# Two output projections and the first tile's normalisation moved into the last two half periods of the attention

## What is computed

```python
mod = (silu(c) @ wmod)                      # six vectors per batch: sa, ca, ga, sb, cb, gb
h = layernorm(x) * (1 + ca) + sa
x = x + ga * (causal_attention(h @ wq, h @ wk, h @ wv, rotary, 32 heads of 32) @ wo)
h = layernorm(x) * (1 + cb) + sb
g = softmax(h @ W_gate.T) - 0.125 * sigmoid(h @ W_thr + b_thr)   # 8 experts
w = where(g >= 0, g, 0); w = w / sum(w)
y = h @ W_base.T + b_base + 2 * einsum('ner,ne,eor->no', h @ A_w, w, B_w)
x = x + gb * y
```

## Time and profile before

| | us |
|---|---|
| median of 3 runs (1678.32 to 1681.45) | 1680.01 |
| the profiled execution: its own time | 1680.86 |
| its span, first to last instruction | 1679.1 |
| TensorE busy (95% of the span) | 1591.7 |
| ScalarE busy (62%) | 1038.7 |
| VectorE busy (57%) | 965.4 |
| Pool busy (36%) | 606.3 |

### The profile page before, as it was taken

How to read it: one execution, slowest core, us unless ns; L and a number is a source line. 1 busy time by engine, 2 the same in 40 slices (tenths; PEclk the granted TensorE clock), 3 DMA queues, 4 the chain that set the end, 5 groups by cost and what they waited for, 6 DMA issues and landing times.

```text
span 1679.1 us, 29431 instructions
## 1 busy us (share of the span) xinstructions
PE 1591.7 (95%) x9530; PEld 1179.7 (70%) x9530; DVE 965.4 (57%) x2916; ACT 1038.7 (62%) x2672; POOL 606.3 (36%) x475
## 2 busy tenths in 40 slices
PE   4899999999999989999999999998789999999996
PEld 2556767667677757777777777764468888888885
DVE  5627577676766646666566557565544545453533
ACT  2347888889889868898898898888621111110100
POOL 3533253453533414334234233231314343434332
PEclk9999999999999989999999999996999999999998
DMA  9673443445433383243233323323641212111110
GB/s 350 217 252 86 110 106 104 123 119 139 117 98 97 75 266 88 58 105 77 74 89 75 91 70 92 78 49 99 171 141 38 75 44 69 51 63 60 53 62 25
DMA packets 172163, 174.44 MB, mean 104 GB/s; under 512 B 21172, under 2 KB 120804, under 8 KB 172024
## 3 DMA queue, kind: packets, MB, share of 16 engines
q1 hardware_dynamic: 169912, 168.55, 35.8%
q10 hardware_dynamic: 2112, 4.19, 0.8%
HBM read 96.65 MB, written 25.18 MB: 73 GB/s over the span
## 4 chain that ended last, share of the span: by engine, by line
PE 80%; DVE 6%; DMA 4%; ACT 4%; issue 3%; POOL 2%; SPq 1%; DVEq 0%; ACTq 0%; POOLq 0%
PE ps_s L1224 14%; PE ps_qkv L1224 13%; PE ps_s L687 10%; PE ps_s L1266 9%; PE ps_pv L1293 9%; PE ps_t L1235 8%; PE ps_s L648 3%; PE ps_s L649 3%; PE ps_s L650 3%; DVE rows_sb L1742 1%; PE ps_qkv L689 1%; DMA x_start<-in_L_attn_x_dram 1%; PE ps_s L1137 1%; ACT probsT L1511 1%; DVE h_pair L1711 1%
## 5 line engine op out<-in xcount | busy, mean ns | idle before, releaser
L1475 ACT ACTIVATE rows_sb<-rows_sb,bias_m 128x640 f32<-128x640 f32 (+7 forms) x512 | 396.1, 774 | 12.4
L1742 DVE CUSTOM_DVE_ANT_0 rows_sb<-ps_t,mask 128x512 f32<-128x512 f32 (+3 forms) x512 | 296.7, 586 | 165.1 <-PE ps_t L1235 157.7
L1511 ACT ACTIVATE probsT<-ps_s 128x512 f32<-128x512 f32 (+2 forms) x640 | 320.9, 542 | 26.3 <-PE ps_s L1266 13.5
L1235 PE MATMUL ps_t<-stk 96*128 96x512 f32 (+3 forms) x768 | 270.2, 355 | 11.6 <-DVE smax L1742 7.8
L1266 PE MATMUL ps_s<-stk 98*128 98x512 f32 (+3 forms) x768 | 230.7, 381 | 7.8 <-ACT probsT L1511 7.4
L1768 DVE TENSOR_TENSOR ps_s<-ps_s,mask_t 128x128 f32<-128x128 f32 (+1 forms) x384 | 120.8, 340 | 170.7 <-PE ps_s L1266 166.8
L1266 PEld LDWEIGHTS ps_s<-stk 98*128 98x128 f32 x768 | 129.9, 193 | 93.0 <-issue 50.5
L1235 PEld LDWEIGHTS ps_t<-stk 96*128 96x128 f32 x768 | 147.4, 192 | 62.8 <-DVE smax L1742 14.4
L1293 PE MATMUL ps_pv<-probsT,v_all 128*32 128x256 f32 (+1 forms) x2816 | 185.0, 357 | 0.9 <-ACT probsT L1511 0.9
L1896 POOL TENSOR_TENSOR rope_b<-rope_b,rope_sin 128x512 f32<-128x512 f32 x64 | 82.8, 1294 | 282.6 <-DVE rope_b L1727 282.6
L1224 PE MATMUL ps_qkv<-hT_hi,w_hi 128*128 128x512 f32 x384 | 159.1, 414 | 12.0 <-DMA hT_lo<-h_scratch 6.8
(11 more groups left out here) (212 smaller groups left out, 3046.0 us busy)
## 6 DMA issues: line engine op xcount, KB each, us to landing
stk<-rot SPq DMA_DIRECT2D x384, 128.0 KB, 2.4
probsT<-in_L_wmod_dram SPq DMA_DIRECT2D x5, 2048.0 KB, 10.6
wm_one<-in_L_wmod_dram SPq DMA_DIRECT2D x5, 2048.0 KB, 14.3
w_raw<-in_L_attn_wq_dram SPq DMA_DIRECT2D x16, 512.0 KB, 4.1
w_raw<-in_L_attn_wk_dram SPq DMA_DIRECT2D x16, 512.0 KB, 4.8
w_raw<-in_L_attn_wv_dram SPq DMA_DIRECT2D x16, 512.0 KB, 4.1
attn_scratch<-attn_sb SPq DMA_DIRECT2D x128, 64.0 KB, 3.0
h_scratch<-h_pair SPq DMA_DIRECT2D x32, 256.0 KB, 3.0
```

The source lines that it names most:

```text
L1235: pe.matmul(bank[:, 0:c1 - c0], stk[0:3 * HD, u % 2, 0, qt // 4, h, qt % 4 * P:(qt % 4 + 1) * P], stk[0:3 * HD, u % 2, 1, part, h, 0:c1 - ...
L1475: act.activation(row, row, ACT.Exp, bias=bias_m[:, qt, h:h + 1], scale=SCALE, accum_out=sums[:, qt // 4, h, qt % 4:qt % 4 + 1]).then_inc(s ...
L1511: act.activation(probsT[:, w % 4, hs[0]:hs[-1] + 1, 0:n], s_bank[(NS * u + k) % 3][:, 0:len(hs) * n].rearrange("p (h n) -> p h n", h=len(hs)),
L1742: dve.tensor_tensor_reduce(rows_sb[:, to, at + c0:at + c1], bank[:, 0:n], mask[:, BANK - n:BANK] if last else mask[:, 0:1].broadcast_to([P ...
```

## The change

- Projection 0 stands in six steps, (30, 6) to (30, 11), 8 matmuls each, projection 1 in nine, (31, 3) to (31, 11). Tile 0's residual stands at the end of (31, 2) on VectorE, its normalisation at (31, 4), its transposition at (31, 10) on TensorE.
- Pool alone splits Wo, in one block of cast and subtraction for each k, then also casts the first two tiles of attention output. ScalarE does nothing of it.
- Wo's transfers, the attention output of tiles 0 and 1, `ga` and the rows of x are issued earlier, at new places in SyncE's queue.
- Behind the attention stand the 14 pieces, and tile 0's two feature halves between them.
- The transfers of batch 1 have a semaphore for each feature half, and a chain waits for the half that it reads.
- Banks of PSUM and places in SBUF are shared out anew; the residual's product is two instructions of 512 columns instead of one of 1024, for each tile.

```diff
-WO_AT = {(PAIRS - 2 + k // 4, (4, 5, 8, 9, 1, 2, 6, 8)[k]): k for k in range(KT)}
...
+        def load_ga(sp):
+
+            sp.wait_ge(wo_lo_ok, KT)
             sp.wait_ge(gate_st, 16)
             for b in range(B):
                 sp.dma_start(ga[:, b, :], gate_dram[b:b + 1, :].broadcast_to([P, D])).then_inc(rows_ld, 16)
...
-            project(0, lambda: turn_weights(pe, 0))
-            turn_weights(pe, 1)
...
-            project(1, rest_and_xn)
+            for part in range(2):
+                turn_weights(pe, part)
+            pe.wait_ge(st_hi, UNITS)
+            pe.wait_ge(st_lo, UNITS)
             tile_loops(pe, body)
...
-            split_weights(0)
-            split_a(act, 1)
-            split_weights(1)
-            split_weights(2)
-            split_h(0)
+            for half in range(2):
+                split_h_half(0, half)
+                split_weights(half)
...
-            split_a(0)
-            split_a(1)
+            for i in range(2):
+                pool.wait_ge(a_ld, 16 * i + 16)
...
+                if i:
+                    pool.wait_ge(wo_ok, i)
+                pool.tensor_copy(a_hi[:, :, :], a_raw[:, :, :]).then_inc(a_hi_ok, 1)
+                split_a(i)
...
                 if u == PAIRS - 2:
-                    for k in range(2, 4):
-                        load_wo(k)
+                    load_wo(5)
+                    load_wo(6)
+                if u == PAIRS - 1:
+                    sp.wait_ge(sum_ok, NW * PAIRS)
+                    for e in range(2):
+                        load_x1(sp, e, e)
                 if p and t + 3 < T:
                     load_w(0, t + 3)
                 if u + 1 < PAIRS:
                     place_m(u + 1, 0)
                 if u == 2 * G - 3:
                     load_next_hT(1)
+                if u == PAIRS - 3:
+                    sp.wait_ge(rope_mul, 4 * T)
+                    load_a(sp, 0)
+                    load_wo(2)
+                    load_wo(3)
+                if u == PAIRS - 2:
+                    load_wo(7)
...
                 if u == PAIRS - 2:
-                    load_a(sp, 0)
+                    load_ga(sp)
+                    sp.wait_ge(a_lo_ok, 1)
+                    load_a(sp, 1)
...
-                        pe.wait_ge(hT_ld[c], 16 * 4)
+                        pe.wait_ge(hT_ld[c][kt // 4], 32)
...
+                    if u == PAIRS - 2 and i >= 6:
+                        if i == 6:
+                            pe.wait_ge(vT_ok, 2 * T)
+                            pe.wait_ge(wo_hi_ok, KT)
+                            pe.wait_ge(wo_lo_ok, KT)
+                        project(pe, 0, 8 * (i - 6), 8 * (i - 5))
+                    if u == PAIRS - 1 and i >= 3:
+                        project(pe, 1, 6 * KT * (i - 3) // 9, 6 * KT * (i - 2) // 9)
                     if u == PAIRS - 1 and 0 < i <= SOON:
-                        turn_weights(pe, 2 + i)
+                        turn_weights(pe, 1 + i)
+                    if u == PAIRS - 1 and i == SOON + 2:
+                        pe.wait_ge(st_lo, SOON)
+                        turn_xn(pe, 0)
...
+            def split_wo():
+
+                pool.wait_ge(proj_mm, 6 * T)
+                for k in range(KT):
+                    pool.wait_ge(wo_ld[k % 2], 16 * (k // 2 + 1))
+                    pool.tensor_copy(wo_hi[:, k, :], wo_raw[k % 2]).then_inc(wo_hi_ok, 1)
+                    pool.wait_ge(wo_hi_ok, k + 1)
+                    pool.tensor_tensor(wo_lo[:, k, :], wo_raw[k % 2], wo_hi[:, k, :].bitcast(F32),
+                                       ALU.subtract).then_inc(wo_lo_ok, 1)
```

More of the change, by code:

```diff
@@ L397, in adaln_block @@
         h_st = sem("h_st")
-        hT_ld = [sem("hT_ld0"), sem("hT_ld1")]
+        hT_ld = [[sem(f"hT_ld{c}_{half}") for half in range(2)] for c in range(2)]
         pool_half = sem("pool_half")
@@ L642, in rest_weights, with three, project @@
                 dve.tensor_tensor(lo, turns, hi.bitcast(F32), ALU.subtract).then_inc(st_lo, 1)
[L644 to L652 removed]
+        def three(pe, out_ap, hi, lo, w_hi_ap, w_lo_ap, first, final):
+            pe.matmul(out_ap, hi, w_hi_ap, start=first, stop=False)
+            pe.matmul(out_ap, hi, w_lo_ap, start=False, stop=False)
+            return pe.matmul(out_ap, lo, w_hi_ap, start=False, stop=final)
+        def project(pe, j, m0=0, m1=6 * KT):
+            if m0 == 0:
                 pe.wait_ge(a_hi_ok, j + 1)
@@ L657, in project, with turn_xn, phase_b_tensor @@
                     pe.wait_ge(gated, j)
[L658 to L674 removed]
+            for m in range(m0, m1):
+                c, kt, way = m // (3 * KT), m // 3 % KT, m % 3
+                mm = pe.matmul(q_bank[c], (a_hi, a_hi, a_lo)[way][:, kt, :],
+                               (wo_hi, wo_lo, wo_hi)[way][:, kt, c * BANK:(c + 1) * BANK],
+                               start=m % (3 * KT) == 0, stop=m % (3 * KT) == 3 * KT - 1)
+            if m1 == 6 * KT:
+                mm.then_inc(wo_ok, 1)
+        def turn_xn(pe, j):
+            pe.wait_ge(xn_ok, j + 1)
+            if not isinstance(j, int) or j:
+                pe.wait_ge(h2t_ok, 2 * j)
+            for half in range(2):
+                for q in range(4):
+                    kt = 4 * half + q
+                    mm = pe.transpose(ps_t[half][:, q * P:(q + 1) * P], xn[:, kt * P:(kt + 1) * P], ident[:, :])
+                mm.then_inc(xt_ok, 1)
+        def phase_b_tensor(pe):
             def body(hp, e, b, bj, has_next, has_next2):
@@ L755, in split_weights, with residual, norm @@
                         "p (k n) -> p k n", k=4)).then_inc(st_hi, 1)
-            split_weights(0)
-            split_a(act, 1)
-            split_weights(1)
-            split_weights(2)
-            split_h(0)
-            tile_loops(act, body)
+            for half in range(2):
+                split_h_half(0, half)
+                split_weights(half)
+            tile_loops(act, body)
+        def residual(dve, j, hp, e, b):
+            dve.wait_ge(wo_ok, j + 1)
+            if not isinstance(j, int) or j:
+                dve.wait_ge(xt_ok, 2 * j)
+                dve.wait_ge(out_ok, j)
+            for c in range(2):
+                cols = slice(c * BANK, (c + 1) * BANK)
+                part = dve.tensor_tensor(xn[:, cols], q_bank[c], ga[:, b, cols], ALU.mult)
+            part.then_inc(gated, 1)
+            dve.wait_ge(gated, j + 1)
+            dve.wait_ge(x_ld[e], 16 * hp + 16)
+            dve.tensor_tensor(x1[:, e, :], x1[:, e, :], xn[:, :], ALU.add).then_inc(x1_ok, 1)
+            dve.wait_ge(x1_ok, j + 1)
+            for c in range(2):
+                st = dve.bn_stats(stats[:, c, :], x1[:, e, c * BANK:(c + 1) * BANK])
+            st.then_inc(bn_ok, 1)
+            own(dve)
+            dve.wait_ge(bn_ok, j + 1)
+            dve.bn_aggr(mv[:, 0, :], stats[:, :, :].rearrange("p a s -> p (a s)")).then_inc(b_st, 1)
+        def norm(dve, j, e):
+            dve.wait_ge(b_rs, j + 1)
+            dve.tensor_scalar(xn[:, :], x1[:, e, :], mv[:, 0, 0:1], rstd[:, 0:1], ALU.subtract,
+                              ALU.mult).then_inc(xn_ok, 1)
         def phase_b_vector(dve):
@@ L804, in modulate @@
[L804 removed]
+                    modulate_half(j, b, half)
             def route(i):
@@ L1833, in _ @@
                         rope_products(*ROPE_AT[u, i])
+                    if u == PAIRS - 1 and i == 2:
+                        dve.wait_ge(rows_ld, 16 * B)
+                        residual(dve, 0, 0, 0, 0)
+                    if u == PAIRS - 1 and i == 4:
+                        norm(dve, 0, 0)
             phase_b_vector(dve)
```

198 lines of the change are left out of this document (70 added, 128 removed).

## The result

| | before | changed |
|---|---|---|
| median of 16 runs, us | 1678.32 | 1688.18 |
| lowest and highest | 1674.83, 1681.45 | 1682.31, 1693.6 |
| span of the profiled execution | 1679.1 | 1687.6 |
| mean granted clock | 0.978 | 0.970 |

The changed kernel takes 1.0057 times as long (95% interval 1.0046 to 1.0068): 9.6 us, between 7.7 and 11.4. The forecast was slower, 1684.8 us with a range of 1674 to 1692. The median lies in the range, but the loss is twice the +4.8 us of the sum: the sign and the range held, the size didn't. The spans differ by 8.5 us, and this is the number that can be taken apart.

A forecast was written before the change was run, and what follows sets the result against it. Exponentials and waits between engines bound half period 30, TensorE having room; the tail waited for transfers. -3.5 + 0 + 13.4 + 7.9 + 10.5 - 26.0 + 2.5 = +4.8 us, giving 1684.8 us, range 1674 to 1692.

The forecast's parts named there:

- batch 1 in halves: Where batch 1 begins: TensorE's wait ends when the first half has landed, -3.5 us.
- up to (30, 6): Ahead of step (30, 6): ScalarE loses a Wo cast, -1.05, VectorE's maxima meet Pool's subtractions, +1; sum 0.
- the wait at (30, 6): Ahead of the first projection matmul: TensorE waits for the row's issue, Wo's eighth block and Pool's work, +13.4 us.
- the rest of half period 30: Behind that wait: TensorE becomes the bound with 48 added matmuls and a low clock, 21.9 us against 14.05, +7.9.
- half period 31: TensorE's work with the matmuls, a 5.0 us wait for x and piece 1, and the clock: 34.9 against 24.40, +10.5.
- between attention and tiles: The tail: only 14 pieces are left, 13.7 us instead of 39.7, -26.0.
- into the tile loop: First tile: gates and bias load late, uncovered, so VectorE reaches the transposition after TensorE; +2.5 us, ends 0 and 4.
- the slower rival's first half: In the wait at (30, 6): Pool's cast costs as much as its subtraction, +2.6 us; the whole rival, 1689.2, chance 0.13.
- The faster rival: Half period 31: SyncE's queue is ahead, x lands in time, -6.5, tail pieces in place, -2.7: 1675.6 us, chance 0.20.
- the 12 to 15 given as a sign: Tail: the time from TensorE's last values to the first tile should be 12 to 15 us.
- the two meetings: In (29, 6) and (30, 1): VectorE's maxima meet Pool's subtraction, can lose 1.8 us each, partly hidden, +1.

The follow-up runs named there:

- e3: Changed kernel with the eighth Wo block issued ahead of the row of maxima and Pool's attention-output cast and subtraction ahead of its sixth Wo block: 1680.79 us.
- e11: Changed kernel with only the eighth Wo block issued ahead of the row of maxima; one run, trace only: the 12.79 us wait falls by 5.04.
- e12: Changed kernel with only Pool's attention-output cast and subtraction ahead of its sixth Wo block; one run, trace only: the 12.79 us wait falls by 3.27.
- e2_x_early: Changed kernel with the rows of x issued at the head of half period 31, ahead of the second row of maxima and a store: 1681.4 us.
- e8_split_p1: e7 with projection 1 cut: 21 matmuls stay in half period 31, 18 go into the tail, 9 behind the last piece: 1663.72 us.
- e4: Changed kernel with VectorE's and Pool's wait for gates and bias moved from the tile loop's head to their first use: 1688.07 us.
- e6: Changed kernel with the edits of e3, projection 0 begun two steps later, and the early x of e2_x_early: 1671.08 us.
- e7: e6 with the late wait for gates and bias of e4: 1665.99 us.
- e1_halves: Kernel before, with only the semaphore for each feature half of batch 1: 1675.17 us, 0.9978 of before.

## Why the prediction was right, and where its sum was not

| step of the sum | predicted | measured |
|---|---|---|
| batch 1 in halves | -3.5 | -3.75 (6.84 to 3.09) |
| up to (30, 6) | 0 | -0.45 |
| the wait at (30, 6) | +13.4 | +13.2 |
| the rest of half period 30 | +7.9 | +7.9 (21.93 for 14.05) |
| half period 31 | +10.5 | +12.3 (36.74 for 24.40) |
| between attention and tiles | -26.0 | -24.6 (15.15 for 39.72) |
| into the tile loop | +2.5 | +5.1 (436.14 for 431.08 up to the end) |
| sum | +4.8 | +9.7 |

**The sign and the mechanism held.** The first four steps are right to within half a microsecond each, though for the second that is luck, as said below. The wait at (30, 6) was certain from the order of the instructions, and e3, e11 and e12 showed both of its links, the queue and Pool's share. Its terms came as written: the row's issue began 1.0 us behind T (I had 1.1), block 8 was with Pool 3.7 us behind its own issue (4.0), and Pool needed 6.85 us (6.91). Pool's cast takes 1.04 us, as its copy of the same size and not as its subtraction, so the slower rival's first half is out.

**Half period 31 was sized 1.8 us too low.** The wait behind piece 1 is 5.23 us where I had 5.0, but x came later than I had it: it was issued 6.4 us after the half period's start (I had 5.3), and VectorE had it 4.5 us later (I had 4.0). The wait is hardly longer for it, because TensorE came later as well, 10.2 us after the start (I had 9.2). The sum has no term for projection 1's first matmul, which reuses the banks that VectorE must first multiply: 1.18 us at 1206.30. The faster rival, SyncE's queue being ahead, was the mechanism of e2_x_early: there x had landed when VectorE had made the product, and that gave 6.0 us against the rival's 6.5.

**The tail was sized 1.4 us too low.** It was costed at full clock and ran at 0.77: the twelve transpositions behind the wait of 3.14 us took 3.03 us, while the twelve at its start, at 1236.31, took 1.44. ScalarE then waited for TensorE ahead of each of the last casts, which came 0.85 us apart:

```profile
1249.48 0.58 ACT L751 CAST wb_hi<-ps_s 128x512 fp32r<-128x512 f32 x1 [0.27 <-PE ps_s L633]
```

With matmuls in place of the wait, in e8_split_p1, the tail ran at 1.00. That the clock makes up the whole 1.4 us is argued from these rows and not shown by a run of its own. Its loads landed in 3.8 and 4.3 us, where the sum has 4.5 "as above" (above stands 4.0, between 3.3 and 4.8). From TensorE's last values to the first tile it is 15.72 us, just over the 12 to 15 given as a sign.

**Into the tile loop is the step that failed most,** by 2.6 us and beyond its end of 4. I let the bias land 6.0 us after its issue, as before; now it took 7.4, and VectorE stood for 8.73 us. DMA issues from 1236 to 1252:

```profile
bias<-in_L_ffn_b_base_dram SPq DMA_DIRECT2D x1, 512.0 KB, 7.4
```

Why it took longer is open. In e4, e6, e7 and e8 it took 7.0 to 7.4 us too, and the attention output's transfer, issued 0.8 us behind it, stood there before as well. VectorE reached the transposition with TensorE 1.30 and 0.47 us early, as the mechanism said, but TensorE had also been slowed. It ran at half clock from 1253.3 to 1256.4 (0.50), behind the tail's last wait, and again from 1270 to 1273 (0.52) behind the 1.77 us. The stretch up to tile 1's transposition took 17.78 us at 0.90 in place of 14.03 at 1.00, 3.75 us, and 1.3 us more went behind it. I had no term for the clock in either place, only in the two half periods. The experiments part the 5.1 us: without the wait at the loop's head 3.5 go (e4_late), and without the waits in the tail 1.7 (e7_comb_late to e8_split_p1), so the bias was under-sized by about 1 us and the clock behind the tail, which the sum put at nothing, was worth 1.5 to 1.7.

**The step up to (30, 6) came out by luck.** The 0.45 us in the table is within the 2.2 us by which the same code differs there from trace to trace (e1_halves). And the two meetings for which I had +1 didn't happen. In (29, 6) and (30, 1) the column of maxima came at the end of Pool's cast, ahead of its subtraction, and took 0.16 us; it met a subtraction in (30, 6), the one place that was slow before and that the sum doesn't count, and only at its end:

```profile
1128.32 0.16 DVE L1772 SCALAR_TENSOR_TENSOR m_col<-logs,smax 128x8 f32<-128x8 f32 x1
1148.13 0.16 DVE L1772 SCALAR_TENSOR_TENSOR m_col<-logs,smax 128x8 f32<-128x8 f32 x1
1162.55 0.41 DVE L1772 SCALAR_TENSOR_TENSOR m_col<-logs,smax 128x8 f32<-128x8 f32 x1
```

Pool's subtraction of 1160.57 ends at 1162.94, and VectorE's instruction at 1162.96. Before, the two ended at 1168.40 and 1168.42, in e1_halves at 1164.82 and 1164.84, and in e3_wo_both, where VectorE's instruction met a cast of Pool and took 0.94 us, at 1148.76 and 1148.78. What it costs depends on when the two meet: 0.25 us here, where the earlier trace rows had 1.8. No row told when they would meet, so the term was a chance and not a sum.
